# A gather waits for the gather two places ahead of it, with two landing semaphores per slot

## The reference

```
h    = relu(layernorm(x))                         # [12500, 128], no scale or shift
msgs = for each edge e:  h[src[e]] @ W[type[e]] + b[type[e]]     # W [4,128,128], b [4,128]
out  = x + segment_sum(msgs, dst)                 # [12500, 128]
```

## Time and profile before

| | us |
|---|---|
| median of 3 runs | 2284.09 |
| the profiled execution | 2289.54 |
| its span, first to last instruction | 2287.8 |
| GpSimd busy | 1477.3 |
| TensorE matmuls busy | 1023.3 |
| VectorE busy | 672.9 |
| ScalarE busy | 149.9 |

### The profile page before, as it was taken

The page is one execution under the profiler, slowest core; times in us unless marked ns, Lnnn a source line. Parts: engine busy times, 40 slices in busy tenths (PEclk is TensorE's granted clock), DMA queues, the critical chain, the costliest instruction groups (busy, mean ns, idle before and its releaser), DMA issues.

```text
span 2287.8 us, 18293 instructions
## 1 busy us (share of the span) xinstructions
PE 1023.3 (45%) x4086; PEld 704.6 (31%) x4087; DVE 672.9 (29%) x1535; ACT 149.9 (7%) x399; POOL 1477.3 (65%) x1573
## 2 busy tenths in 40 slices
PE   5774243334444444444444444444444444443234
PEld 2232233223232323232323232333233333233234
DVE  5554123133232323232323232323232323121123
ACT  3341000000000000000000000000000000000000
POOL 6666666656666666666666666666666666666663
PEclk9886566666666666666666666666666566655566
DMA  8663111111111111111111111111111111111241
GB/s 249 220 206 111 45 46 44 48 37 45 47 45 47 45 47 45 47 45 47 45 47 45 47 45 47 45 48 45 47 45 46 45 47 45 47 45 45 69 116 43
DMA packets 95392, 144.22 MB, mean 63 GB/s; under 512 B 27481, under 2 KB 57683, under 8 KB 95363
## 3 DMA queue, kind: packets, MB, share of 16 engines
q0 software_dynamic: 50016, 102.50, 17.1%
q1 hardware_dynamic: 40567, 38.92, 5.2%
q10 hardware_dynamic: 4780, 2.51, 0.4%
HBM read 111.73 MB, written 32.09 MB: 63 GB/s over the span
## 4 chain that ended last, share of the span: by engine, by line
POOL 40%; issue 28%; PE 13%; another core or an unknown queue 12%; DVE 3%; DVEq 2%; DMA 1%; ACT 0%; SPq 0%; ACTq 0%; POOLq 0%
POOL messages L367 32%; POOL lists L367 8%; PE ps_sum L815 6%; PE ps_y L773 3%; PE ps_y L839 2%; DVE lists L641 1%; PE ps_y L832 0%; DVE stage L553 0%; PE ps_sum L764 0%; DVEq L661 0%; DVE acc L632 0%; DVE stats L493 0%; DMA lists<-in_dst 0%; DVE ps_node L670 0%
## 5 line engine op out<-in xcount | busy, mean ns | idle before, releaser
L367 POOL DMA_INDIRECT messages<-message_table,table_row x1155 | 1090.0, 944 | 559.5 <-issue 336.1
L815 PE MATMUL ps_sum<-messages,lists 128*128 128x128 f32 x1776 | 353.7, 334 | 440.5 <-issue 407.4
L815 PEld LDWEIGHTS ps_sum<-messages,lists 128*128 128x128 f32 x1776 | 298.3, 238 | 480.9 <-issue 479.3
L632 DVE SCALAR_TENSOR_TENSOR acc<-ps_sum,own_tile,acc x203 | 70.4, 347 | 1112.9 <-remote 1037.6
L367 POOL DMA_INDIRECT lists<-message_table,table_row x288 | 271.8, 944 | 154.2 <-issue 83.0
L815 PE MATMUL ps_sum<-messages,onehot 128*128 128x128 f32 x582 | 132.1, 363 | 274.0 <-issue 256.6
L641 DVE SCALAR_TENSOR_TENSOR lists<-ps_node,node_iota,dst_col 128x1024 f32<-128x1024 f32 x148 | 190.0, 1284 | 114.4 <-issue 55.9
L815 PEld LDWEIGHTS ps_sum<-messages,onehot 128*128 128x128 f32 x582 | 114.8, 269 | 302.3 <-issue 302.2
L815 PE MATMUL ps_sum<-lists 128*128 128x128 f32 x592 | 127.3, 358 | 143.3 <-issue 132.1
L839 PE MATMUL ps_y<-stage 128*128 128x512 f32 x136 | 116.9, 896 | 146.5 <-issue 111.4
L353 POOL DMA_INDIRECT early_x<-in_x,src_col x119 | 112.6, 946 | 65.8 <-issue 33.0
(11 more groups left out here) (89 smaller groups left out, 580.6 us busy)
## 6 DMA issues: line engine op xcount, KB each, us to landing
message_table<-stage SPq DMA_DIRECT2D x98, 256.0 KB
messages<-message_table,table_row POOLq DMA_INDIRECT x1155
out<-acc SPq DMA_DIRECT2D x24, 256.0 KB
lists<-message_table,table_row POOLq DMA_INDIRECT x288
acc<-in_x SPq DMA_DIRECT2D x4, 896.0 KB
early_x<-in_x,src_col POOLq DMA_INDIRECT x119
acc<-in_x ACTq DMA_DIRECT2D x2, 896.0 KB, 5.8
acc<-in_x SPq DMA_DIRECT2D x1, 832.0 KB
```

The costliest lines, as they stand in the source:

```text
L367: pool.indirect_dma_start(messages[k][0:rows, t, :], None, table_rows, bass.IndirectOffsetOnAxis(ap=flat_rows[0:rows, at + t:at + t + 1], ...
L632: ins = nc.vector.scalar_tensor_tensor(out=rows, in0=sums, scalar=mine[:, bass.ds(place, 1)], in1=rows, op0=ALU.mult, op1=ALU.add)
L815: ins = nc.tensor.matmul(ps_sum[:, bass.ds(q % BANKS, 1), 0:d], onehots[k][:, t, :], messages[k][:, t, :], start=(t == 0), stop=(t == tile ...
```

## The change

Each slot has two landing semaphores, one for its even and one for its odd tiles, where it had one. Ahead of every gather but the first two, GpSimd waits until the gather two places ahead of it, counted over slots and rounds, has landed. TensorE waits for both semaphores of a slot where it waited for one. What is gathered, in which order and by how many instructions, is as before.

```diff
+IN_FLIGHT = 2
...
-    gathered = [sem(f"gathered{k}") for k in range(SLOTS)]
+    gathered = [[sem(f"gathered{k}_{t}") for t in range(IN_FLIGHT)] for k in range(SLOTS)]
...
                 for t in range(tiles):
                     rows = edge_tail if at + t == full_edge_tiles else P
+                    before = i * (SLOTS * SB_TILES) + k * SB_TILES + t - IN_FLIGHT
+                    if before >= 0:
+                        before_sb, before_tile = divmod(before, SB_TILES)
+                        pool.wait_ge(gathered[before_sb % SLOTS][before_tile % IN_FLIGHT],
+                                     (before_sb // SLOTS * SB_TILES + before_tile) // IN_FLIGHT * 16 + 16)
                     pool.indirect_dma_start(
                         messages[k][0:rows, t, :], None, table_rows,
-                        bass.IndirectOffsetOnAxis(ap=flat_rows[0:rows, at + t:at + t + 1], axis=0)).then_inc(gathered[k], 16)
+                        bass.IndirectOffsetOnAxis(ap=flat_rows[0:rows, at + t:at + t + 1], axis=0)).then_inc(gathered[k][t % IN_FLIGHT], 16)
...
-            def superblock(s, k, tiles, needed, release_slot=True):
+            def superblock(s, k, tiles, rounds_before, release_slot=True):
                 windows, regs = load_windows(pe, s)
                 with pe.Fori(0, windows):
                     q = pair()
-                    pe.wait_ge(gathered[k], needed)
+                    for n in range(IN_FLIGHT):
+                        pe.wait_ge(gathered[k][n], rounds_before * (16 * SB_TILES // IN_FLIGHT) + 16 * len(range(n, tiles, IN_FLIGHT)))
                     pe.wait_ge(pair_added, q)
                     pe.wait_ge(onehot_ready, q)
...
-                    superblock(EARLY_SBS + i * SLOTS + k, k, SB_TILES, (i + 1) * (16 * SB_TILES))
+                    superblock(EARLY_SBS + i * SLOTS + k, k, SB_TILES, i)
...
-            superblock(full_sbs, 0, last_tiles, rounds * 16 * SB_TILES + 16 * last_tiles, False)
+            superblock(full_sbs, 0, last_tiles, rounds, False)
```

## The result

The changed kernel takes 2327.35 us (median of 4, from 2325.86 to 2329.08), the kernel before 2286.84 us (median of 4, from 2275.62 to 2304.51). The ratio is 1.017, with an interval of 1.0103 to 1.0237: 1% to 2.4% slower. The forecast was no change. A repeat (experiment 5) gave 1.0100 [1.0069, 1.0132]. So the change is slower by 1% to 2%.

The account below looks back on a forecast made before the run. GpSimd's gather queue was taken to set the time, with pauses following a hidden 1.395 us per gather. Waits absorbed 0, smaller edits 0, last windows 1 us gave 2290.5 us, less 5.5 for the median: 2285 us, range 2228 to 2350.

Parts of the forecast that it names:

- the first rival: Gather stage: the waiting isn't absorbed and every wait is added, 45 us, giving 2330 us (2300 to 2380); chance 0.24.
- Landing and notice of two gathers: GpSimd's wait ahead of each gather: 2.38 to 2.63 us for two, taken as 1.28 each, 45 us of new waiting.
- The second wait at a slot's first gather: GpSimd has two waits there, 181 times: between nothing and 0.305 us each, 0 to 55 us, covered, so 0.
- The cover: Pauses in the gather stage shrink by what the waits take, as long as a gather stays under 1.395 us: 0 us.
- Slots come free late: Gather stage: back-to-back gathers starve TensorE and VectorE, so GpSimd stops at the next slot boundary; 68 pauses, 266 us between.
- 0 us for the middle way: Gather stage at 1.28 us per gather, under 1.395: new waits and shorter pauses cancel, 0 us; chance 0.42.
- the law: Gather stage: a run with its pause ends after 1.395 us per gather plus 0.62 us, 34.1 us for 24 gathers.
- The last windows: After the last gather, 29.3 us: TensorE's one more wait in some seven windows, at most 2 us, taken as 1 us.
- starvation ends: Gather stage: with waits, the other engines are no longer starved; 1.28 us per gather, -221 us, 2064 us; chance 0.09.
- Starvation recedes: Gather stage: slots are free in time, pauses left out, 1.395 us per gather, 2013 us, -55 us, 2230 us; chance 0.14.
- The wait never holds: Waits ahead of gathers: landing and notice take 2.38 us each time, the change does nothing, 2285 us; chance 0.06.
- landing counts from the end of the record: Waits ahead of gathers: 3.32 us for two gathers, 1.66 each, stage 2395 us, kernel 2612 us; chance 0.05.

Follow-up runs that it names:

- experiment 5: The changed kernel again, unedited, on another chip, against the kernel before: 2322.39 us, ratio 1.0100.
- experiment 8: Changed kernel with one gather in flight, each waiting for the one just ahead of it: 4327.64 us (one run).
- experiment 2: Changed kernel with four gathers in flight, each waiting for the one four places ahead: 2304.89 us, ratio 0.9995 to the kernel before.
- Experiment 3: Changed kernel with the two waits at a slot's first gather exchanged, landing first, slot second: 2304.21 us, ratio 0.9986 to the kernel before.
- experiment 4: Changed kernel with the landing wait ahead of tile 4 of each slot alone: 2327.56 us, ratio 1.0104 to the kernel before.
- 7: Changed kernel with the landing wait ahead of tiles 3 and 6 of each slot alone: 2342.63 us, ratio 1.0161 to the kernel before.
- 6: Changed kernel with the landing wait ahead of tiles 2, 4 and 6 of each slot alone: 2363.29 us, ratio 1.0248 to the kernel before.
- experiments 11: Changed kernel with the landing wait ahead of the odd tiles of each slot alone: 2314.93 us, ratio 1.0042 to the kernel before.

## Where the prediction held and where it failed, step by step

The measured 2327.35 us lie inside the range of 2228 to 2350 us, but not in the forecast's own 2262 to 2300, and the one sum that comes near, the first rival's 2330, stands on a mechanism that did not happen. It is luck that the time lies in the range: two large terms, 317 us of new waiting and 266 us of pauses gone, nearly cancel. The forecast had 45 us for each of them.

**Landing and notice of two gathers: too small.** This is the term that decided. The prediction bounded it at 2.38 to 2.63 us and took 1.28 us for each gather. It is 2.78 us with one in flight (experiment 8) and 2.81 in the changed kernel, 1.405 for each gather outside a slot's start. The bounds were made from the packets and a product's notice. The 0.33 us from the last packet to the last increment were in neither. The step matters more than its size tells: 1.405 lies beyond the 1.395 us that the prediction itself named as the point up to which waits are absorbed, and 1.28 lay below.

**The second wait at a slot's first gather: priced at nothing, worth up to 85 us.** The bounds were 0 and 0.305 us each and both too low. Experiment 8 has it at 0.48 us. 180 times 0.47 is 85 us. Together with the step before, 1443 x 1.405 + 85 = 2112 us, and the stage measured 2118.0. What costs is not that there are two waits (satisfied ones are free, experiment 2), but that the landing wait, the one that ends last, is the one that stands alone. Experiment 3 exchanges the two and gets 1.1% back.

**The cover: right in kind, used up.** Pauses end by the count of gathers and not by the time since they were issued: 34.3 to 34.5 us for most runs of 24 with no wait, with three waits (experiment 4), with half the rows and half the bytes. In the changed kernel all pauses are gone, (2.728 - 1.249) x 180 = 266 us. The waits take 196.5 us inside the slots and (1.919 - 1.249) x 180 = 120.6 us at their starts, 317 us, which is 51 us more than the cover. Given that the stage's 2067 us had 1443 x 1.395 = 2013 of the hidden service, there was by this estimate at most about 54 us to gain from regular spacing, and none at a spacing above 1.433.

**"Slots come free late": wrong.** The prediction read the pauses as GpSimd waiting for a TensorE that is starved and behind. The slots had been freed 28.8 us (median) before the increment that GpSimd waited for arrived. So what catches up with 1.395 us for each gather is not TensorE's work but, as the events have it, the arrival of such increments. In the changed kernel, with 1.469 us for each gather, most of them arrive at once.

**0 us for the middle way: wrong, by a part that stays open.** Experiments 4, 7 and 6 hold back few enough gathers to stay under 1.395 (1.292, 1.325, 1.359 us) and lose 1.0, 1.6 and 2.5%, because runs appear that are longer than the law. The increments of `slot_free` are as late there as before (29.0, 28.3 and 29.7 us at the pauses, medians), but why some runs end 4 to 14 us after the law stays open. In experiments 11 and 3 (1.41 us) pauses are fewer, 21 and 16, and the kernel is level with the one before again, within 0.4%.

**The last windows: 1 us more forecast, 17.6 us less measured.** The prediction took the 29.3 us after the last gather as fixed. They go with the pauses: 24 instead of 89 passes are left after the last gather, and 11.7 us of 29.3.

**The rivals.** The number came near to the first one (2330), but its mechanism did not happen: it kept every pause and added the waits, while in truth every pause went; and its reason, slow passes that TensorE still has to make, falls with the slots that had long been free. What did happen to TensorE is what "starvation ends" described: the distances of 0.70 and 1.40 us are gone. It was given 0.09 and had the time wrong, 2064 us, since it needed 1.28 us for each gather, and no kernel here has been seen below 1.40 us without pauses. "Starvation recedes" had one sign come true, runs longer than 48 gathers and then no pause at all; its time of 2013 us for the stage did not, as the spacing of 1.469 us in the mean was beyond 1.395. "The wait never holds" and "landing counts from the end of the record" fall with experiment 8: the latter needed 3.32 us for two gathers, where 2.81 were measured.

Of the signs that the prediction listed, the one against its bound came: idle time per gather outside 0.27 to 0.37 us (1.405 - 0.944 = 0.46 in a slot). Runs longer than 48 gathers, its sign against its reading of the starvation, came too.

## What to carry to other kernels

Price a wait on a DMA by the distance of two transfers with one in flight, not by when the last packet starts: here 2.78 us, where last packet (2.18) and notice (0.26) make 2.44. Where an instruction has two waits, look in the trace which one stands alone, and write first the one that is satisfied last, so that it rides on the instruction: here that was worth 1.1% of the kernel. Where a wait's releaser is "remote", look for the instruction that gives the signal before calling its engine slow: here it had ended 29 us earlier. And where an engine pauses after a count of its own transfers, issuing faster gained nothing, as with half the rows; issuing slower gained nothing either, it was level within 0.4% at a pace of 1.41 us and lost 1 to 2% at 1.47.

## What the runs showed of the hardware

- The 16 increments of a gather's semaphore are complete some 0.33 us after its last packet starts.
- A wait that stands alone ahead of a gather on GpSimd costs 0.47 to 0.5 us more than one that rides on it, after the moment at which it is satisfied (experiment 8: 3.27 and 2.78 us; experiment 3: pauses end 0.76 us after the increment, elsewhere 0.26).
- While gathers follow one another at 1.25 us, a matmul's semaphore increment takes effect up to 42 us after the matmul's end (median 16 us for `slot_free`, 28.8 at the pauses); at 1.47 us after 0.01 us (median; at most 4.5 us in the changed kernel, 12 in experiment 5).
- In the same stretches TensorE issues a matmul or a weight load every 0.70 or 1.40 us (1240 us of the stage of before, 21 us in the changed kernel).
- GpSimd's pauses end when, since the last one, 1.395 us for each gather (and mostly 0.6 to 1.4 us) have passed, some runs later. This is independent of the bytes (102.50 and 55.23 MB in the queue) and of the rows (128 and 64), 34.1 to 34.5 us for most runs of 24 gathers in each. There are 68 pauses at 1.25 us, 21 and 16 at 1.41 us, none at 1.47.
- The traces keep 16% of the gathers' semaphore increments at a distance of 1.25 us, 77% and 65% at 1.47, all at 2.8.
- 64 row numbers instead of 128 shorten GpSimd's gather from 0.944 to 0.905 us only, and its distance from 1.249 to 1.21 us.
- No kernel here ran the stage at less than 1.43 us a gather, pauses included: by catching up, or by waiting for landings. Fewer gathers that bring more rows each weren't tried.
